# Score matmuls in 32- and 64-row groups of TensorE, and the first maxima moved beside the layer before

## The reference, cut to what matters

```python
# layer 1: 32 score heads of width 4 (16 differential heads), causal
s = jnp.einsum('bhqd,bhkd->bhqk', q, k) * scale
s = jnp.where(mask, s, jnp.finfo(s.dtype).min)
p = jax.nn.softmax(s, axis=-1)
return jnp.einsum('bhqk,bhkd->bhqd', p, v)
# layer 2: 16 heads of width 8, no mask
scores = jnp.einsum('bhqd,bhkd->bhqk', Q, K) / np.sqrt(Hd).astype(jnp.float32)
attn = jax.nn.softmax(scores, axis=-1)
out = jnp.einsum('bhqk,bhkd->bhqd', attn, V)
```

## Time and profile before

| | |
|---|---|
| median of 3 runs | 1531.0 us |
| profiled execution | 1529.98 us |
| its span | 1528.2 us |
| PE busy | 1342.3 us (88%) |
| DVE busy | 970.2 us (63%) |
| ACT busy | 665.5 us (44%) |
| mean granted TensorE clock | 0.899 |

### The profile page before, as it was taken

How to read it: one execution, slowest core, us unless ns; L and a number is a source line. 1 busy time by engine, 2 the same in 40 slices (tenths; PEclk the granted TensorE clock), 3 DMA queues, 4 the chain that set the end, 5 groups by cost and what they waited for, 6 DMA issues and landing times.

```text
span 1528.2 us, 23814 instructions
## 1 busy us (share of the span) xinstructions
PE 1342.3 (88%) x9318; PEld 812.0 (53%) x9334; DVE 970.2 (63%) x2093; ACT 665.5 (44%) x1424; POOL 203.0 (13%) x189
## 2 busy tenths in 40 slices
PE   7977788998897787888989989999779899999999
PEld 4455657876765674343756656654334323234565
DVE  3568743343453677876877876465667888876365
ACT  2444143753541431023433435666446566666621
POOL 1132170000202300035000000044100100000000
PEclk8988698998996987569999999999989999999988
DMA  8000123341000310015253363211212303000000
GB/s 248 6 1 1 29 67 100 98 113 49 27 1 14 70 22 3 0 41 146 89 130 109 107 168 120 92 45 29 64 20 53 64 5 66 3 1 28 1 8 21
DMA packets 65100, 86.22 MB, mean 56 GB/s; under 512 B 9566, under 2 KB 49374, under 8 KB 63326
## 3 DMA queue, kind: packets, MB, share of 16 engines
q1 hardware_dynamic: 60892, 76.30, 19.1%
q0 software_dynamic: 4096, 8.40, 2.0%
HBM read 62.19 MB, written 22.48 MB: 55 GB/s over the span
## 4 chain that ended last, share of the span: by engine, by line
PE 64%; DVE 14%; DMA 8%; ACT 4%; issue 4%; POOL 3%; SPq 2%; DVEq 0%; ACTq 0%
PE psA L404 32%; PE psB L404 25%; PE psB L408 5%; DVE mx L1485 3%; POOL slots_x L1922 2%; PE psA L408 2%; ACT pbuf L1738 2%; DMA wA<-slots_x 2%; POOL tH L1935 1%; DVE st L1168 1%; ACT pbuf L1820 1%; DMA arena<-scr1k 1%; DMA scr1k<-arena 1%; DMA arena<-slots_x 1%; DMA arena<-scr2k 1%
## 5 line engine op out<-in xcount | busy, mean ns | idle before, releaser
L1820 ACT ACTIVATE pbuf<-psA 128x512 f32<-128x512 f32 (+3 forms) x768 | 350.0, 489 | 250.2 <-PE psA L404 243.1
L1485 DVE TENSOR_REDUCE mx<-psA 128x1 f32<-128x512 f32 (+3 forms) x608 | 377.7, 657 | 101.2 <-PE psA L404 97.2
L404 PE MATMUL psA<-arena 64*64 64x128 f32 (+9 forms) x1632 | 243.2, 308 | 14.0 <-DVE mx L1485 11.1
L404 PEld LDWEIGHTS psA<-arena 64*64 64x64 f32 (+3 forms) x1632 | 131.5, 138 | 115.2 <-DVE mx L1485 44.2
L1738 ACT ACTIVATE pbuf<-psA,st,rq 128x128 f32<-128x128 f32 x256 | 92.7, 467 | 112.8 <-DVE st L1172 112.8
L404 PE MATMUL psA<-arena,w 96*128 96x512 bf16 (+4 forms) x320 | 114.8, 411 | 19.3 <-DMA arena<-scr2k 10.4
L404 PE MATMUL psA<-w_identb,w_mdiagT 128*128 128x128 bf16 x512 | 110.9, 243 | 0.0
L404 PE MATMUL psA<-w_mdiagT,w_identb 128*128 128x128 bf16 x512 | 110.0, 223 | 0.0
L404 PE MATMUL psB<-xf,wA 128*128 128x128 f32 x624 | 93.8, 295 | 6.1 <-DMA wA<-in_moe 5.7
L404 PE MATMUL psB<-pbuf,arena 128*5 128x512 f32 (+3 forms) x1024 | 95.3, 445 | 0.4 <-ACT pbuf L1820 0.4
L1935 POOL DMA_INDIRECT tH<-slots_y,slot_i x64 | 62.0, 968 | 237.7 <-DMA slots_y<-tH 219.3
(11 more groups left out here) (295 smaller groups left out, 2136.2 us busy)
## 6 DMA issues: line engine op xcount, KB each, us to landing
wA<-in_moe SPq DMA_DIRECT2D x39, 576.0 KB, 3.8
wA<-in_moe SPq DMA_DIRECT2D x39, 256.0 KB, 3.0
slots_x<-wA SPq DMA_DIRECT2D x20, 256.0 KB, 3.7
slots_y<-tH SPq DMA_DIRECT2D x18, 256.0 KB, 3.6
wA<-slots_x SPq DMA_DIRECT2D x15, 256.0 KB, 4.1
arena<-scr2k SPq DMA_DIRECT2D x48, 64.0 KB
scr1q<-arena SPq DMA_DIRECT2D x4, 384.0 KB, 4.0
scr1k<-arena SPq DMA_DIRECT2D x4, 384.0 KB, 4.1
```

The lines of the kernel that those rows point to most:

```text
L404: return pe.matmul(out, lhsT, rhs, start=start, stop=stop, skip_group_check=True)
L1485: dv.tensor_reduce(m[:, t, h:h + c], topb("mx", lay, b, n)[:, 0:c * k].rearrange("p (c k) -> p c k", c=c), AX.X, ALU.max) \
L1820: ac.activation(pb(lay, b, s, j)[:, 0:T - q0_], scoreb("ex", lay, b, s, j)[:, 0:T - q0_], ACT.Exp, bias=0.0, scale=1.0) \
```

## The change

It has these parts.

1. The stacks are laid out in row groups. In layer 1 each group of 8 score heads has its own 32 partitions (24 rows of parts, 3 rows of maxima), in layer 2 each group of 8 heads has 64 (48 and 3). A score matmul reads only its group: 24 or 27 rows of a 32-row group in layer 1, 48 or 51 rows of a 64-row group in layer 2. The orders of heads (`tops_of`, `tile_of`, `HO`) change so that neighbouring steps are in different groups.
2. The mask goes first (`start`), in one matmul for a whole `mx` step, and the score matmuls are added to it.
3. The rows of ones are no longer loaded: GpSimd sets the whole key stack to ones (`clr`), and the loads overwrite the other rows. The stacks come back in 48 DMAs in layer 1 and 24 in layer 2, the maxima in 4 and 2 where there was 1. The key stack of layer 1 is a quarter of its size and that of layer 2 a half in columns.
4. `mx` of layer 1's batch 0 uses the bank `accY` for odd and `misc` for even steps, and no longer waits for layer 0's end; `MERGE` puts 43 of its 88 steps between the windows of layer 0's last batch and the other 45 behind its last projection.
5. `pb` has 12 tiles where it had 8, `pv` and `tail` are a stream of their own (k), and `MERGE` is new as a whole.

```diff
+        def maxb(lay, b, n):
+            return topb if (lay, b) != (1, 0) else accY if n % 2 else misc
-        pb = Ring(ptiles)
+        pb = Ring(ptiles + [arena[:, 7680 + T * k:8192 + T * k] for k in range(4)])
-        HR = {1: 108, 2: 102}
+        HS = {1: 32, 2: 64}
+        HO = {1: (0, 1, 2, 3), 2: (0, 2, 1, 3)}
+        def q_of(lay, i, h, rows):
+            p = HS[lay] * (h // 8)
+            return HQ[lay][i][p:p + 6 * HD[lay] + rows, h % 8, :]
+        def k_of(lay, i, h, rows):
+            p = HS[lay] * (h // 8)
+            return HK[lay][i][p:p + 6 * HD[lay] + rows, h % 8 // 4 if lay == 1 else h % 8, :]
...
             def mx(lay, b, n):
-                if (lay, b, n) == (1, 0, 0):
+                if (lay, b, n) == (1, 1, 0):
                     pe.wait_ge(*y_n.at(3, 7, 1))
                     pe.wait_ge(*xadd.at("wo", 3, 1))
                 pe.wait_ge(*stack_in[b].at(lay))
-                for h, t, o in tops_of(lay)[n]:
-                    m = mm(bank[:, o:o + k], HQ[lay][i][0:96, h % 8, t * P:(t + 1) * P], HK[lay][i][0:96, kof(lay, h), 0:k],
-                           True, not CAUSAL[lay])
-                    if CAUSAL[lay]:
-                        m = mm(bank[:, o + k - P:o + k], mdiagT, identb, False, True)
+                if CAUSAL[lay]:
+                    mm(bank[:, 0:c * k].rearrange("p (c k) -> p c k", c=c)[:, :, k - P:k], mdiagT,
+                       identb.unsqueeze(1).to_broadcast([P, c, P]), True, False)
+                for h, t, o in part:
+                    m = mm(bank[:, o:o + k], q_of(lay, i, h, 0)[:, t * P:(t + 1) * P], k_of(lay, i, h, 0)[:, 0:k], not CAUSAL[lay], True)
...
             def ex(lay, b, s, j):
-                m = mm(bank[:, 0:T - q0_], HK[lay][i][0:HR[lay], kof(lay, g), kb * P:(kb + 1) * P],
-                       HQ[lay][i][0:HR[lay], g % 8, q0_:T], True, not causal)
                 if causal:
-                    m = mm(bank[:, 0:P], identb, mdiagT, False, True)
-                m.then_inc(*ex_mm.up(lay, b, s, j))
+                    mm(bank[:, 0:P], identb, mdiagT, True, False)
+                mm(bank[:, 0:T - q0_], k_of(lay, i, g, 3)[:, kb * P:(kb + 1) * P], q_of(lay, i, g, 3)[:, q0_:T], not causal, True) \
+                    .then_inc(*ex_mm.up(lay, b, s, j))
...
+                for j in range(P // HS[lay]):
+                    r, rows = HS[lay] * j, slice(HS[lay] * j, HS[lay] * j + HS[lay])
+                    for part, n in ((0, 3), (1, 2), (2, 1)):
+                        qs = dr["q"][b][part, rows].rearrange("(i g) c -> i g c", g=8)
                         for k in range(n):
+                            sy.dma_start(HQ[lay][i][r:r + D], qs).then_inc(*stack_in[b].up(lay))
+                            ks = dr["k"][b][k, rows].rearrange("(i g) c -> i g c", g=8)
+                            if lay == 1:
+                                ks = ks.rearrange("i (h r) c -> i h r c", h=2)[:, :, j, :]
+                            sy.dma_start(HK[lay][i][r:r + D], ks).then_inc(*stack_in[b].up(lay))
+                            r += D
```

More of the change, by code:

```diff
@@ L25 @@
 EPS32 = float(np.finfo(np.float32).eps)
+ONE2 = float(np.array([0x3F803F80], np.uint32).view(np.float32)[0])
 MERGE = (
[L28 to L31, removed]
@@ L805, in mx @@
                 u = "mx", lay, b, n
-                for w in topb.free(*u):
+                for w in maxb(lay, b, n).free(*u):
                     pe.wait_ge(*w)
-                if (lay, b, n) == (1, 0, 0):
+                if (lay, b, n) == (1, 1, 0):
                     pe.wait_ge(*y_n.at(3, 7, 1))
@@ L1989, in stored @@
                 tH.give(("y", lay, q), ys_out[q].now())
[L1991 to L2002, removed]
             def stack(lay, b):
@@ L2047, in mxT @@
                 sy.wait_ge(*part_m[b].at(lay))
-                sy.dma_start(HQ[lay][i][96:HR[lay], :, :], dr["m"][b].rearrange("s (j g) c -> (s j) g c", g=8)) \
-                    .then_inc(*max_in[b].up(lay))
+                for j in range(P // HS[lay]):
+                    r = HS[lay] * j + 6 * HD[lay]
+                    sy.dma_start(HQ[lay][i][r:r + 3], dr["m"][b][:, 8 * j:8 * j + 8, :]).then_inc(*max_in[b].up(lay))
             def wi3_():
@@ L2110, in streams @@
                 main += [("kn0", b, kv) for kv in range(4)] + [("v0", b, j) for j in range(4)] + [("sc", b, i) for i in range(8)]
+            take = []
             for lay in (1, 2):
@@ L2113, in streams @@
                 for b in four:
+                    main += [("ex", lay, b, s, j) for s in range(last_) for j in range(4)]
                     for s in range(last_):
-                        for j in range(4):
-                            main.append(("ex", lay, b, s, j))
-                            if j == 1 and s:
-                                main.append(("pv", lay, b, s - 1))
-                        if s and s % 4 == 0:
-                            main.append(("tail", lay, b, s // 4 - 1))
-                    main += [("pv", lay, b, last_ - 1), ("tail", lay, b, last_ // 4 - 1)]
-                    main += [("cmb1", b)] * (lay == 1) + [("pj1", lay, b), ("pj2", lay, b)]
+                        take += [("pv", lay, b, s)] + [("tail", lay, b, s // 4)] * (s % 4 == 3)
+                    take += [("cmb1", b)] * (lay == 1) + [("pj1", lay, b), ("pj2", lay, b)]
             ffn = together("h1") + [("qkv0", b, k) for b in four for k in range(3)]
@@ L2159, in streams @@
                         mix += [("yv", b, i - 1, x)] * (0 < i < 9) + [("tp", b, i, x)] * (i < 8)
-            return [norm, main, ffn, stack, top] + flows + [mix]
+            return [norm, main, ffn, stack, top] + flows + [mix, take]
         def merged():
@@ L2168, in merged @@
                 else:
-                    order += [next(todo["abcdefghij".index(c)]) for _ in range(int(n or 1))]
+                    order += [next(todo["abcdefghijk".index(c)]) for _ in range(int(n or 1))]
                     n = ""
@@ L2265, in constants @@
     c["selq1"], c["selk1"] = c["selq1"].astype(np.float32), c["selk1"].astype(np.float32)
-    one = np.zeros((3, 4, 8, T), np.float32)
-    for h in range(8):
-        one[:, h % 4, h] = 1
-    c["kone1"] = bf(one.reshape(12, 8, T))
-    one = np.zeros((3, 2, 16, T), np.float32)
-    for h in range(16):
-        one[:, h // 8, h] = 1
-    c["kone2"] = bf(one.reshape(6, 16, T))
     c["hsel"] = (i[:, None] // 8 == np.arange(16)[None]).astype(np.float32)
```

125 lines of the change are left out of this document (57 added, 68 removed).

## The result

| | kernel before | changed kernel |
|---|---|---|
| time, us (median, range, runs) | 1529.1 (1524.9 to 1532.3, 4) | 1856.5 (1843.4 to 1868.5, 4) |
| ratio, 95% interval | | 1.214 (1.205 to 1.223) |
| profiled execution, time / span | 1530.0 / 1528.2 | 1843.4 / 1841.6 |
| granted clock over the span | 0.90 | 0.78 |

The account below looks back on a forecast made before the run. PE bounds layer 1, about 87% full and waiting for almost nobody. From 1530.0 us: -24 first maxima, +10 moved steps, +12 batch 0 stall, +107 layer 1, +8 and +2 stack loads, -7 layer 2 = 1638 us; range 1572 to 1680.

Parts of the forecast that it names:

- Layer 1: +107 us: Layer 1: 1498 more changes of array shape at 0.09 us make 135 us, partly hidden by gaps; net +107, bounds +75 and +135.
- rival (c): Layer 1: SP's queue becomes the bound, stacks late by 15 us, clock falling in the waits; 1678 us, chance 0.09.
- a sign of being wrong: Layer 1: prediction wrong if 32-row matmuls follow masks without a gap, or its length doesn't follow the number of changes.
- The price and the count of a change: PE: each change of array shape costs 0.09 us; the count goes from 268 to 1766, 1498 more.
- Rival (a): Score matmuls: row groups overlap and a change of shape into another group costs nothing; 1514 us, faster, chance 0.12.
- rival (b): Layer 1: half of the drains are hidden in PE's gaps; layer 1 +55, total 1586 us, chance 0.09.
- The first maxima: Block behind layer 0: 45 of 78 steps stay, at 0.74 us each, 33 us instead of 57.7, so -24.
- +10 and +12: Layer 0's last windows: +10 for 33 moved maxima steps, a third hidden; +12 for PE's wait on batch 0's stack loads.
- the stall: Before batch 0's first maxima in layer 1: PE waits 12 us for the stack loads, bounds 0 and +20.
- the stack of batch 1: Layer 1's batch 1: 48 small loads issue more slowly and PE waits for them, +5 us.
- Layer 2: Layer 2: overlap of 64-row score matmuls -18, 120 more changes of shape +11; net -7, bounds -25 and +8.

## Why the prediction was wrong

**The step that failed: the clock.** "Layer 1: +107 us, bounds +75 (all short gaps go) and +135" is made of durations at 2.4 GHz, and the forecast put nothing on a fall of the clock there. It used 1.2 GHz for the block of maxima, and as a bound on one change (0.14 us); only rival (c) has a clock that falls, in waits for loads. Whether short scores and many changes would move the clock where it had been full was not asked. In layer 1 half clock took 167 us instead of 12, and in the whole span 183 us more. It is also what the prediction named as a sign of being wrong, that layer 1's length doesn't follow the number of changes: 553 and 654 us with the same 633. No range drawn from rows at full clock could hold that. Rows that could have raised the question were there: the earlier trace rows has a clock of 0.50 where PE runs short bursts between reductions, and of 0.95 where it is full, and the change puts some 1500 stops into the full stretch. That few rows count too stood in no row of the trace before. The Trainium skill (TensorE: Matmul & The Clock Gate, "A second HAM failure mode: psum-queue depth-cycling") describes a kernel in which PE idles briefly between groups of matmuls so often that its clock swings between full and half. The kernel with masks over 64 rows is like it, though its stops are changes of shape: 1615 more of 0.11 us in layer 1, and the clock at 0.83 instead of 0.96.

**The price and the count of a change: right, a little low in price.** 0.09 us was forecast; the median in the changed kernel's trace is 0.109 us into 32 rows and 0.103 out of them at full clock, 0.112 and 0.108 at half. In layer 1 (705 to 1186 against 737 to 1483 us) 1345 more changes added 149 us, 0.11 each, and 31 us of gaps went with them, net +118, where the step said +107. Rival (a), a free change, is refuted, and rival (b), half of the drains hidden, too: 31 of 149 is a fifth. The Trainium skill's sentence that a new tiling mode drains TensorE (TensorEngine Tiling (Array Packing), Tiling Modes, Key Properties) agrees with the medians here, 0.10 to 0.11 us into and out of 32 and 64 rows, also where only the rows differ.

**The first maxima: right in kind, too good in size.** The block is 41 us (624 to 665), not 33: -17 instead of -24. 45 steps at 0.91 us each are above the 0.82 us that was the upper bound; 90 changes cost 10.5 us in it, and the clock is 0.62. Before it, the stretch from 530 us grew from 74 to 94 us, +20, where +10 and +12 were forecast. Within that the stall is larger, 23.1 instead of 12, beyond its bound of 20, because the 48 issues take 27.6 us on SP's queue and not 16.3: a small one takes 0.46 or 0.61 us, not the 0.34 taken from a run of six.

**Behind the block, 665 to 737 us:** 72 us instead of 43, +29 where +5 was forecast for the stack of batch 1. The longer issue is 13.9 us of wait; half clock is 16 us instead of 5, and 86 changes cost 10.

**Layer 2: wrong sign.** -7 was forecast, +16 came. The overlap was sized well: 25 us of columns, where -18 was taken and -25 the bound. The changes were 192 more and not 120, +22 us. Half clock took 19 more. The bound of +8 did not hold, in part for the same reason as in layer 1, in part for the count. That 64-row groups in layer 2 alone lose 2.3% says that this part does not pay here.

**The sum again**, by stretch: 530 to the end of the shortened block +20 and -17, behind it +29, layer 1 +265, layer 2 and the rest +16, together +313. The direction was right for the reason given, the stops, which are 200 of the 313 us. Less the 183 us of half clock the loss would have been 130, near the forecast's 108.

What stays open: whether few rows and stops are one cause of the lower clock, and how they add up in the changed kernel (no run kept its 24- and 27-row scores and its masks in one shape at once); and where the moved maxima's 8 us come from.

## What to carry to other kernels

Price a change of TensorE's array shape (rows or columns) at the 0.10 to 0.11 us each way that the medians here have, count them along the instruction order, and ask for each stretch at full clock whether the change makes the array stop often or leaves its rows idle: here that cost nearly as much again as the stops (183 and 200 us). In this kernel row groups overlapped only where their products stood side by side in different groups, with no whole-array matmul between them, and in layer 2, where they did, the kernel was still 2.3% slower. Giving the scores the mask's few rows saves most stops but not the clock (still 9 to 10% longer over 32 rows, 5% over 64); reading all groups at once in layer 1 saved both, and left the waits for loads. Many small loads on a shared queue are a cost of their own.

## What the runs showed of the hardware

- The granted clock was lower the fewer rows the matmuls used. With the same matmuls and 633 changes, layer 1's clock was 0.87 at 64 rows and 0.70 at 32. That had not been expected: a product of 512 columns over 24 rows is under way for 0.38 us at full clock, as one over 102 is.
- A change that only shortens the contraction, with no tile moved, costs what any other does: into 64 rows 0.108 us, out of them 0.106, medians of some 690 and 610 changes at full clock in the kernel with masks over 64 rows.
- Small loads cost their issuer 0.46 to 0.62 us each on SP's queue when they alternate between two destinations.
- The same chip executed the kernel before in 1651 us and half an hour later in 1532, so "chips differ" in the expectations does not explain the two levels. A reduction of 512 columns takes 0.685 us at either level; the longer execution has single waits that the other lacks, as these of PE (who for whom, us, times, longest):

```profile
PE psA L404 <- DVE pbuf L1192: 19.5, 3, 18.0
...
PE psA L404 <- ACT pbuf L1820: 21.4, 4, 18.9
```

Their cause was not looked into.
